# Two attention layers in one kernel: the plan of row-maximum jobs in the global layer's main stage, streams one behind the other

## What is computed

```python
x = x + _L0_conv_ref(_gn(x), ...)   # x: 16 images, 32x32, 192 channels
x = x + _L1_conv_ref(_gn(x), ...)
# L0
scores = q @ jnp.swapaxes(k, -1, -2) * SCALE + attn_bias   # rel_h + rel_w
attn = jax.nn.softmax(scores, axis=-1)
out = attn @ v
# L1
scores = jnp.where(mask_cat[None, None], scores, NEG_INF)
attn = jax.nn.softmax(scores, axis=-1)
```

## Time and profile before

| | |
|---|---|
| median of 3 runs | 4869.68 us (4855.43 to 4874.59) |
| profiled execution, its own time | 4862.39 us |
| its span, first to last instruction | 4860.6 us |
| TensorE, VectorE, ScalarE, GpSimd busy | 91%, 63%, 53%, 18% |
| mean granted TensorE clock | 0.967 |

### The profile page before, as it was taken

The page is one execution under the profiler, slowest core; times in us unless marked ns, Lnnn a source line. Parts: engine busy times, 40 slices in busy tenths (PEclk is TensorE's granted clock), DMA queues, the critical chain, the costliest instruction groups (busy, mean ns, idle before and its releaser), DMA issues.

```text
span 4860.6 us, 97545 instructions
## 1 busy us (share of the span) xinstructions
PE 4446.6 (91%) x32598; PEld 2268.6 (47%) x32598; DVE 3079.8 (63%) x5558; ACT 2594.1 (53%) x3955; POOL 892.4 (18%) x1901
## 2 busy tenths in 40 slices
PE   4879999999999999999999999999999999999988
PEld 3334453544535454453544535454453544535434
DVE  3736667666675756657566675756757566675644
ACT  1533556555564655555555565555546555565564
POOL 4122021222202222021222202222031221202111
PEclk7988999999999999999999999999999999999999
DMA  6333152442514433153442424433253432424402
GB/s 123 87 73 77 44 119 64 100 87 56 107 42 107 88 89 75 44 115 68 100 80 58 101 52 103 91 83 75 45 114 75 100 80 49 103 60 100 88 15 40
DMA packets 235869, 386.05 MB, mean 79 GB/s; under 512 B 58396, under 2 KB 133728, under 8 KB 235360
## 3 DMA queue, kind: packets, MB, share of 16 engines
q1 hardware_dynamic: 189280, 266.13, 23.7%
q10 hardware_dynamic: 21504, 75.51, 7.8%
q0 software_dynamic: 24576, 37.80, 4.9%
HBM read 227.79 MB, written 88.08 MB: 65 GB/s over the span
## 4 chain that ended last, share of the span: by engine, by line
PE 71%; DVE 11%; issue 6%; DMA 5%; SPq 5%; ACT 2%; DVEq 0%; ACTq 0%; POOL 0%
PE P L1143 14%; PE P L1161 13%; PE P L1102 12%; DVE mx L909 7%; PE P L966 5%; PE P L967 5%; PE P L1193 4%; PE P L1214 4%; DMA queries<-oraw 4%; PE P L1110 3%; PE P L1079 3%; SPq L514 3%; DVE mxc L915 2%; PE P L1186 1%; PE P L1231 1%
## 5 line engine op out<-in xcount | busy, mean ns | idle before, releaser
L909 DVE TENSOR_REDUCE mx<-P 128x1 f32<-128x512 f32 x3072 | 1921.3, 684 | 457.4 <-PE P L1102 453.3
L779 ACT ACTIVATE probs<-P 128x1024 f32<-128x1024 f32 x1536 | 1507.5, 1022 | 854.0 <-PE P L1161 853.8
L1102 PE MATMUL P<-K,AR 96*128 96x256 f16 x6144 | 1074.1, 278 | 56.6 <-DMA AR<-biases 29.5
L1161 PE MATMUL P<-AR,K 113*128 113x512 f16 x3072 | 924.9, 383 | 13.2 <-DMA AR<-mrow 12.6
L915 DVE TENSOR_REDUCE mxc<-P 128x1 f32<-128x336 f32 (+1 forms) x1536 | 656.3, 474 | 317.9 <-PE P L1111 315.0
L1143 PE MATMUL P<-probs,V 128*17 128x512 f32 x6144 | 813.5, 601 | 5.7 <-ACT probs L779 5.7
L1102 PEld LDWEIGHTS P<-K,AR 96*128 96x128 f16 x6144 | 532.2, 98 | 581.4 <-DVE mx L909 202.0
L795 ACT ACTIVATE probs<-P 128x320 f32<-128x320 f32 (+3 forms) x1632 | 612.1, 437 | 338.2 <-PE P L1214 268.4
L1161 PEld LDWEIGHTS P<-AR,K 113*128 113x128 f16 x3072 | 213.3, 98 | 670.3 <-ACT probs L779 519.6
L1110 PE MATMUL P<-K,A 112*128 112x320 f16 (+1 forms) x1536 | 405.2, 300 | 68.7 <-DVE mx L909 54.9
L1214 PE MATMUL P<-A,K 113*128 113x320 f16 (+2 forms) x1536 | 428.3, 300 | 14.7 <-ACT probs L795 14.3
(11 more groups left out here) (125 smaller groups left out, 3718.4 us busy)
## 6 DMA issues: line engine op xcount, KB each, us to landing
AR<-biases SPq DMA_DIRECT2D x384, 256.0 KB, 7.9
AR<-queries ACTq DMA_DIRECT2D x96, 512.0 KB, 5.9
biases<-xn SPq DMA_DIRECT2D x128, 256.0 KB, 2.6
AR<-queries ACTq DMA_DIRECT2D x96, 256.0 KB, 8.8
K<-oraw POOLq DMA_DIRECT2D x384, 64.0 KB, 4.7
xin<-in_x_dram SPq DMA_DIRECT2D x16, 768.0 KB, 10.5
queries<-oraw SPq DMA_DIRECT2D x384, 32.0 KB, 4.6
QA<-queries SPq DMA_DIRECT2D x192, 64.0 KB, 2.8
```

Of the source, the lines that this page charges most:

```text
L779: nc.scalar.activation(probs[:, u % RING, j:j + 2, :], P[:, b:b + 2, :], ACT.Exp).then_inc(p_done[0], 1)
L909: V_.reduce_max(mx[:, n // 2, n % 2:n % 2 + 1], bank, AX.X).then_inc(used, 1)
L1102: last = mm(bank[:, QD * (v % 2):QD * (v % 2) + QD], AR[0:ROWS_MAX[0], part % SLOTS, v, c, j, 128 * q:128 * q + 128], K0[0:ROWS_MAX[0], h, ...
L1161: last = mm(P[:, j, :], K0[0:ROWS, h, 128 * kt:128 * kt + 128], AR[0:ROWS, p % SLOTS, kt // 2, :, j, :], start=True, stop=True)
```

## The change

The plan of layer 0's main stage alone. The streams of the three lists used to overlap where one ended and the next began (steps 13 to 20, 27 to 32, 73 to 77). Now each starts where the other ends: phase 2 in steps 0 to 16, local group 0 in 16 to 28, phase 3 in 28 to 44, phase 4 in 44 to 60, phase 5 in 60 to 76, local groups 1 and 2 in 76 to 95. The four `rel` jobs move from steps 8, 11, 14 and 17 to 16, 19, 22 and 25, among local group 0's. The number of jobs, their operations, the banks and all DMAs are the same.

```diff
     if is_image(image, 0):
-        placed = evenly(max_jobs(0, image, 1), 0, 13) + evenly(max_jobs(0, image, 2), 13, 28)
+        placed = evenly(max_jobs(0, image, 1), 0, 14) + evenly(max_jobs(0, image, 2), 14, 28)
     else:
-        placed = evenly(max_jobs(0, image, 2), 0, 20)
-    placed += evenly(max_jobs(0, image, 3), 27, 45) + evenly(max_jobs(0, image, 4), 45, 61)
-    placed += evenly(max_jobs(0, image, 5), 61, 77)
-    placed += [(8 + 3 * n, job) for n, job in enumerate(rel_jobs(image, 2))]
+        placed = evenly(max_jobs(0, image, 2), 0, 16)
+    for p in (3, 4, 5):
+        placed += evenly(max_jobs(0, image, p), 16 * p - 20, 16 * p - 4)
+    placed += [(16 + 3 * n, job) for n, job in enumerate(rel_jobs(image, 2))]
...
-        placed += evenly(max_jobs(1, i1, 0), 13, 32)
-        placed += evenly(max_jobs(1, i1, 1) + max_jobs(1, i1, 2)[:THIRD], 73, 95)
+        placed += evenly(max_jobs(1, i1, 0), 16, 28)
+        placed += evenly(max_jobs(1, i1, 1) + max_jobs(1, i1, 2)[:THIRD], 76, 95)
```

## The result

The changed kernel takes 4956.18 us, the median of six runs (4939.5 to 4963.15), against 4866.23 for the kernel before in the same measurements. The ratio is 1.0182, with a 95% interval of 1.0161 to 1.0204. The prediction was 4925, and it works out a range of 4890 to 4955: the direction and the place were right, the size was short by 31 us, and the median lies 1 us past the end of that range.

What follows compares the result with a forecast made beforehand. It took TensorE's own issue to bound the kernel, with VectorE close behind. The profiled 4862.4 plus 53 for the 16 blocks and 8 for the clock made 4923, stated as 4925 us, range 4890 to 4955.

Steps and rivals of the forecast that it cites:

- The closing transposes: At layer 0's four stream ends: three maxima and the transpose take 4.1 us, the five-maxima unit behind 3.52.
- Steps 32 to 71: Phases 3 and 4 of a block: +2.5 us against block 8, near 63.2.
- the wait at step 64: TensorE's 0.34 us wait for phase 4's row, in about half the blocks, was to go: -0.4.
- Steps 72 to 95: End of a block: overlap 10.3 us instead of 13.8, later units 26.0 instead of 24.1, sum -1.6, near 36.3.
- Steps 0 to 31: Start of a block, with `rel` jobs among local group 0's: 59.5 us against 57.3, +2.2; bounds 55.3 and 64.
- The clock: More falls to 1.2 GHz in the stretch of long `rel` jobs and TensorE's waits for them: +8 us.
- Rival 1: Every block after the first falls to 1.2 GHz in the new stretch, 15 x 3.1 = 46 us: 4951; chance 0.12.
- Rival 2: A transpose in a unit's second step is cheap, 3.0 us a unit, -70 in all: 4845; 0.12 together with 4.
- 4: Nothing changes, TensorE's issue alone sets the time: within 0.5% of 4870; chance 0.12 together with Rival 2.
- Rival 3: The two overlaps' whole idle time, 4.95 us in each of 15 blocks, comes back and nothing is paid: 4788; chance 0.06.

Runs made afterwards that it cites:

- e1_close_later: The changed kernel with each of layer 0's closing transposes one step later, first in the step where the next stream begins: 4837.11 us, 0.9954 of the kernel before.
- e4_end_only: The kernel before with one part of the change alone, the last local stream from step 77 to 95 instead of 73 to 95: 4859.06 us, ratio 0.9989.
- e2_rel_last: The changed kernel with the four `rel` jobs last in their steps (16, 19, 22, 25) instead of first: 4898.47 us, 1.0072 of the kernel before.
- e7_rows_read: The changed kernel with head group 2's third and fourth `rel` jobs reading queries along rows, not columns (altered computation): 4895.64 us, 1.0068 of the kernel before.
- e6_local_too: The kernel of e5_both_mended with the closing transposes of local groups 0 and 1 one step later too: 4801.74 us, 0.9871 of the kernel before.
- e5_both_mended: The changed kernel with the edits of e1_close_later and e2_rel_last together: 4803.92 us, 0.9866 of the kernel before.

## Why the prediction was right, and where it was short

- **The closing transposes.** Right, in place, mechanism and nearly in size: weights at 3.02 (forecast 3.0), the unit 4.22 (4.1), the one behind 3.5 (3.52). The term of 1.1 for "the transpose and the products with V" measured 2599.03 - 2597.83 = 1.20. Four such units per block, so 0.5 per block and 8 us in all are missing from the sum. e1_close_later shows that the place of the transpose costs, 1.3 in the unit that had it, and that the uneven spread of the maxima that comes with it costs 0.6 in each stream's first unit.
- **Steps 32 to 71.** 63.4 against the forecast's 63.2. The gain of the wait at step 64 that the prediction booked was real: the wait is in no block any more.
- **Steps 72 to 95.** 36.5 against 36.3. The heavier later units were right to be set against the saving in the overlap: e4_end_only has 3.3 of 4.0 given back. But their price was partly luck: six units at 3.01 - 2.59 are 2.5, not the 1.7 of the prediction, which would have made its stretch 0.8 longer. It had each of the two prices from one unit; the nine units together grew by 2.0, against its 1.9.
- **Steps 0 to 31.** 59.8 undisturbed, against 59.5 worked out. Its six units of local and `rel` jobs, which it called the part most likely off, took 5.3, 3.2, 3.9, 6.0, 6.0 and 3.7, against 5.3, 3.3, 3.8, 5.9, 6.0 and 3.7. e2_rel_last shows 2.6 of the block's loss to be the order within the step, the wait for a bank that the prediction named.
- **The clock.** This is the term that was mis-sized: +8 us for more falls. Before, they cost the blocks 1 to 15 some 10 us beyond 57.3 each; now 27 beyond 59.8 each, and more in block 0, whose first stretch grew from 61 to 64. So +17 and up to 2 more, not +8. The 61 of the forecast fell short of the 87 in the spans by 26: some 10 of these are the clock in blocks 1 to 15, 10 the undisturbed steps of those blocks (the 8 of the transposes are most of it), 2 block 0, and 4 lie outside the main stages. The place was right: "in the stretch of long `rel` jobs and TensorE's waits for them". e7_rows_read shows that the falls of steps 22 to 25 need the long jobs. It doesn't show that the waits have no part: with the same long jobs the clock fell in 12 blocks and, where the third job no longer waits in their step (e2_rel_last), in 3. The prediction's reading of the falls before, 1.5 to 3.1 us each, should start at 1.3, block 1's.
- **The rule of the Trainium skill** (TensorE: Matmul & The Clock Gate, "A second HAM failure mode: psum-queue depth-cycling") is that frequent short idle times between groups of products make the clock swing. The fall in every block, which the prediction worked out from it, does not follow for these waits: e7_rows_read has the longer waits and no fall in 14 blocks, and one fall behind waits alone, in block 15.
- **Rivals.** Rival 1's 4951 is nearer to the measured time than the 4925, and for the profiled execution, 4949.49, it is almost exact. That is luck in good part: it had 46 us for the clock in blocks 1 to 15, where the trace has 27, and the steps themselves made up the difference. Its direction was right, not its 3.1 per block. Rival 2 is refuted by the units of 4.22, and 4 by the result. Rival 3's pool of time existed (the overlap of steps 72 to 77 shrinks by 4.0 in e4_end_only), but was given back next door.

Still open: why the clock falls in 12 blocks of the changed kernel and in 5 of e1_close_later, whose `rel` units are the same where it holds. With e4_end_only, where it fell in nine blocks over a plan that was not touched there, and with the 2 and 9 of e6_local_too and e5_both_mended, this says only that the moment counts as well as the content; what in the moment, no run shows.

## What to carry to other kernels

When streams of jobs share in-order engines, look at the one job that needs its whole stream finished, not at the evenness of the plan: put it one score product or more behind the last job it needs, and let a bank be wanted again only in a later step. Here evening out the load alone lost 1.8%, and the same plan with the closing job one step later and the `rel` jobs last in their steps gained 1.3% over the kernel before. Whether the kernel before, with its overlaps and these two mendings, would gain as much was not run. Work moved out of a crowded stretch is priced at what it costs in the stretch that takes it.

## What the runs showed of the hardware

Sixteen products of 64 columns take 0.63 us when their moving operand is read along rows and 2.05 when it is read with a step of 16 elements, and in steps 22 to 25 the granted clock fell only with the second kind: in e7_rows_read TensorE has work in flight for 3.45 of 5.00 us and keeps 2.4 GHz, in the changed kernel for 6.90 of 8.00 and drops to a mean of 0.66. The Trainium skill (SBUF — State Buffer, "Specifications (TRN2)", the row on cachelines) has each access that crosses to a new 16-byte line pay a penalty, which the first half agrees with: a step of 16 elements of two bytes is 32 bytes. Of these two stretches it is the busier one whose clock fell, so the busy time did not tell which would keep it. Slow reads are neither enough (3 of 15 blocks in e2_rel_last) nor always needed (block 15 of e7_rows_read).
